# Running sums of an attention phase: from fp32 matmuls with a copied carry to float32r halves kept in PSUM

## The reference

```python
pos_cos, pos_sin = cos(pos_phases[:L]), sin(pos_phases[:L])
pos_values = x @ Wpv + bpv
pos_ret = (pos_cos * cumsum(pos_cos * pos_values, 1) + pos_sin * cumsum(pos_sin * pos_values, 1)) / sqrt(D)
key_ph = tanh(x @ Wk + bk) * pi
key_cos, key_sin = cos(key_ph), sin(key_ph)
kv_values = x @ Wkv + bkv
gh = gelu(concat([x, shift1(x)], -1) @ Wg1 + bg1)
value_gates = sigmoid(gh @ Wg2 + bg2)
kv_mem_cos = cumsum(shift1(key_cos) * kv_values * value_gates, 1)
kv_mem_sin = cumsum(shift1(key_sin) * kv_values * value_gates, 1)
gate_cumsum = maximum(cumsum(value_gates, 1), 1)
kv_ret = (key_cos * kv_mem_cos + key_sin * kv_mem_sin) / (sqrt(gate_cumsum) * sqrt(D))
bw = softmax(gelu(x @ Wb1 + bb1) @ Wb2 + bb2)
blended = bw[..., 0:1] * pos_ret + bw[..., 1:2] * kv_ret
out = x + layernorm(blended) @ Wo + bo      # normalised again, and added to the input
```

## Time and profile before

| | |
|---|---|
| median of 3 runs | 3560.59 us (3557.9 to 3568.86) |
| profiled execution | 3565.71 us, its span 3563.9 us |
| PE, DVE, ACT, POOL busy over the span | 89%, 87%, 59%, 54% |
| mean granted TensorE clock, as a share of full speed | 0.891 |
| end of the attention phase (first instruction of the next) | 802.83 us |

### The profile page before, as it was taken

One profiled execution on the slowest core, in us unless ns is written; L12 is line 12 of the kernel. 1 busy time (PEld: TensorE's weight loads), 2 busy tenths in 40 slices (PEclk: granted clock), 3 DMA queues, 4 the chain that ended last, 5 costly groups with the idle time before them and its releaser, 6 DMA issues. The chain is left out here.

```text
span 3563.9 us, 91251 instructions
## 1 busy us (share of the span) xinstructions
PE 3177.3 (89%) x31284; PEld 2733.0 (77%) x31284; DVE 3086.5 (87%) x15020; ACT 2120.2 (59%) x4411; POOL 1935.4 (54%) x1758
## 2 busy tenths in 40 slices
PE   5999999972599999999999999999999999999988
PEld 3666666642488888888888888888888888888878
DVE  5666666656999999999999999999999999999971
ACT  3444444422666666666666766666666666766662
POOL 1333333333466666556556666666556656666664
PEclk9999999986699988988888999889998888999988
DMA  2111111103333333333333333333333333333332
GB/s 64 48 54 54 54 54 54 42 30 133 141 117 117 116 105 114 122 105 105 105 105 118 125 119 119 117 108 105 124 112 105 105 105 115 124 124 117 114 117 95
DMA packets 132328, 356.85 MB, mean 100 GB/s; under 512 B 13865, under 2 KB 61609, under 8 KB 129452
## 3 DMA queue, kind: packets, MB, share of 16 engines
q1 hardware_dynamic: 131868, 351.03, 30.3%
HBM read 309.01 MB, written 25.17 MB: 94 GB/s over the span
## 5 line engine op out<-in xcount | busy, mean ns | idle before, releaser
L1209 PE MATMUL b_ps_a<-b_wup,b_hid 128*128 128x256 f32 x4096 | 955.8, 379 | 1.5 <-POOL b_hid L1023 1.5
L1198 PE MATMUL b_ps_h<-b_xT_hi,b_wd_split 128*128 128x256 f32 x4096 | 931.9, 311 | 22.7 <-ACT b_hid L1349 22.5
L1209 PEld LDWEIGHTS b_ps_a<-b_wup,b_hid 128*128 128x128 f32 x4096 | 744.3, 190 | 85.7 <-POOL b_hid L1023 1.7
L1023 POOL TENSOR_TENSOR b_hid<-b_hid,b_gates 128x512 f32<-128x512 f32 x512 | 661.9, 1295 | 197.8 <-ACT b_hid L1349 197.8
L1198 PEld LDWEIGHTS b_ps_h<-b_xT_hi,b_wd_split 128*128 128x128 f32 x4096 | 703.5, 200 | 38.3 <-issue 27.9
L1328 ACT ACTIVATE b_ohq<-b_q_no,b_minus_qid 80x128 f16<-80x128 f16 x2048 | 648.7, 391 | 1.0
L1004 POOL TENSOR_SCALAR b_rstd<-b_mv 128x2 f32<-128x2 f32 x64 | 136.4, 2131 | 860.8 <-DVE b_mv L1388 860.8
L1123 PE MATMUL b_ps_s<-b_ohr,b_ohq 80*128 80x32 f16 x16384 | 452.6, 185 | 167.1 <-issue 125.5
L1198 PE MATMUL b_ps_h<-b_xT_lo,b_wd_split 128*128 128x256 f32 x2048 | 596.9, 291 | 0.0
L1123 PEld LDWEIGHTS b_ps_s<-b_ohr,b_ohq 80*128 80x128 f16 x16384 | 443.8, 102 | 176.0 <-issue 132.3
L1349 ACT ACTIVATE b_hid<-b_ps_h 128x512 f32<-128x512 f32 x512 | 303.8, 593 | 371.5 <-PE b_ps_h L1198 371.3
(11 more groups left out here) (192 smaller groups left out, 5508.8 us busy)
## 6 DMA issues: line engine op xcount, KB each, us to landing
b_wd_split<-wd_parts SPq DMA_DIRECT2D x512, 512.0 KB, 3.8
a_keysh<-a_key SPq DMA_DIRECT2D x16, 896.0 KB, 5.4
a_x<-in_x SPq DMA_DIRECT2D x16, 512.0 KB, 4.9
x_between<-a_y SPq DMA_DIRECT2D x16, 512.0 KB, 3.2
b_x<-x_between SPq DMA_DIRECT2D x32, 256.0 KB, 2.7
wd_parts<-b_wd_split SPq DMA_DIRECT2D x16, 512.0 KB, 2.9
b_x1t<-x_between SPq DMA_DIRECT2D x32, 256.0 KB, 5.5
out<-b_y SPq DMA_DIRECT2D x32, 256.0 KB, 5.6
```

Source lines behind the costliest of these rows:

```text
L1023: G.tensor_tensor(hid[:, p % 4, :, :], hid[:, p % 4, :, :], gates[:, 2 * p:2 * p + 2, :], ALU.mult).then_inc(mix_done, 1)
L1198: mm = T.matmul(hbank[p % 2][:, j * C:(j + 1) * C], a, c, start=i == 0, stop=i == len(parts) - 1)
L1209: mm = T.matmul(abank[:, t * D:(t + 1) * D], hid[:, p % 4, j, t * P:(t + 1) * P], wup[:, 2 * p + j, :], start=p == 0 and j == 0 and t == 0 ...
```

## The change

Six things change, all in `attention_phase`.

1. The sums stay in PSUM. DVE still makes `u`; ACT casts it to float32r (`u_hi`), POOL subtracts to get what is left (`u_lo`, also float32r), and PE adds both halves with a float32r triangle `upto`. The carry is no copy any more: the banks already hold the tile's running sums, and before the next tile a float32r matrix `rest` (ones minus triangle) adds to each row the terms of the tile before that are still missing from it. The banks are started anew only at the head of a sequence. `keep_carry` and `carry` are gone.
2. Chunks go through one sequence and then the other, so `cs` is made for every chunk: 16 times, not 8.
3. The phases are loaded one turn later and first in SP's turn, and `reduce_phases(n + 1)` stands directly ahead of `gate_values(n + 1)`.
4. `terms(n + 1, 0)` and `values(n + 1, 0)` are made at the end of turn `n`, no longer at the start of the next. In ACT's turn the key waves go behind `turn_blend`.
5. `norm_out`, `add_input` and `store` of a chunk move to the next turn. On DVE `norm_out(n - 2)` now stands behind the last `blend` of `n - 1`.
6. The second half of `gate_values` becomes `gate_shares`, behind `back(n, 2)`: three steps for four. `gate_factors` takes two steps for three, and `gate_sums` clamps straight from PSUM.

```diff
-        j, b = divmod(n, seqs)
+        b, j = divmod(n, per_seq)
...
         def sums(n, t):
-            i = g % 2
-            first = j == 0 and t == 0
-            pe.wait_ge(u_done, g + 1)
+            first = g % (per_seq * TA) == 0
+            pe.wait_ge(upto_done, 1)
             if g:
                 pe.wait_ge(prod_done, g)
-            for h in range(2):
-                mm = T.matmul(cbank[h][:, :], tri[:, :], u[:, i, h * 512:(h + 1) * 512], start=True, stop=first)
             if not first:
                 for h in range(2):
-                    mm = T.matmul(cbank[h][:, :], last_row[:, :], carry[:, b, h * 512:(h + 1) * 512], start=False, stop=True)
+                    for part in (u_hi, u_lo):
+                        mm = T.matmul(cbank[h][:, :], rest[:, :], part[:, (g - 1) % 2, h * 512:(h + 1) * 512], start=False, stop=False,
+                                      skip_group_check=True)
+                mm.then_inc(rest_pe, 1)
+            pe.wait_ge(u_lo_done, g + 1)
+            for h in range(2):
+                for part in (u_hi, u_lo):
+                    mm = T.matmul(cbank[h][:, :], upto[:, :], part[:, g % 2, h * 512:(h + 1) * 512], start=first and part is u_hi,
+                                  stop=part is u_lo, skip_group_check=True)
             mm.then_inc(sums_pe, 1)
...
+        def low_terms(n, t):
+            g = n * TA + t
+            i = g % 2
+            pool.wait_ge(u_hi_done, g + 1)
+            G.tensor_tensor(u_lo[:, i, :], u[:, i, :], u_hi[:, i, :].bitcast(F32), ALU.subtract).then_inc(u_lo_done, 1)
...
-        def keep_carry(n, t):
+        def high_terms(n, t):
             g = n * TA + t
-            b = n % seqs
-            act.wait_ge(sums_pe, g + 1)
-            for h in range(2):
-                op = S.copy(carry[96:128, b, h * 512:(h + 1) * 512], cbank[h][96:128, :])
-            op.then_inc(carry_done, 1)
+            act.wait_ge(u_done, g + 1)
+
+            if g >= 2:
+                seq_tiles = per_seq * TA
+                if (g - 1) % seq_tiles == 0:
+                    act.wait_ge(sums_pe, g - 1)
+                else:
+                    act.wait_ge(rest_pe, g - 1 - (g - 1) // seq_tiles)
+            S.copy(u_hi[:, g % 2, :], u[:, g % 2, :]).then_inc(u_hi_done, 1)
...
         def gate_factors(n):
             dve.wait_ge(groot_done, n + 1)
-            V.scalar_tensor_tensor(z[:, :, 1:3], z[:, :, 1:3], 1.0 / 16, den[:, 1, :].unsqueeze(2).to_broadcast([P, TA, 2]),
-                                   ALU.mult, ALU.mult).then_inc(zscale_done, 1)
-            dve.wait_ge(zscale_done, n + 1)
             if n >= 2:
                 dve.wait_ge(blend_done, (n - 1) * TA)
-            V.tensor_copy(fac[:, n % 2, 0, :], z[:, :, 1])
-            V.tensor_tensor(fac[:, n % 2, 1, :], z[:, :, 2], zmax[:, :], ALU.mult).then_inc(fac_done, 1)
+            V.scalar_tensor_tensor(fac[:, n % 2, :, :].rearrange("p c t -> p t c"), z[:, :, 1:3], 1.0 / 16,
+                                   den[:, 1, :].unsqueeze(2).to_broadcast([P, TA, 2]), ALU.mult, ALU.mult).then_inc(zscale_done, 1)
+            dve.wait_ge(zscale_done, n + 1)
+            V.tensor_tensor(fac[:, n % 2, 1, :], fac[:, n % 2, 1, :], zmax[:, :], ALU.mult).then_inc(fac_done, 1)
...
+        def gate_shares(n):
             dve.wait_ge(exp_done, n + 1)
-            V.tensor_scalar(den[:, 0, :], z[:, :, 0], 1.0, None, ALU.add)
-            V.tensor_tensor(den[:, 1, :], z[:, :, 1], z[:, :, 2], ALU.add).then_inc(den_done, 1)
+            dve.wait_ge(constants, 1)
+            V.tensor_reduce(den[:, :, :].rearrange("p c t -> p t c"), z4[:, :, :].rearrange("p t (c k) -> p t c k", k=2), AX.X,
+                            ALU.add).then_inc(den_done, 1)
```

More of the change, by code:

```diff
@@ L138, in attention_phase @@
         sem(f"a_{n}") for n in ("w_high", "xT_hi", "x_before", "tanh", "th_abs", "key"))
[L139 to L143, removed]
+    hidden_done, exp_done, u_hi_done, lnT_done, ph_abs_done, cs_done = (
+        sem(f"a_{n}") for n in ("hidden", "exp", "u_hi", "lnT", "ph_abs", "cs"))
+    xT_pe, keys_pe, hidden_pe, logits_pe, gcum_pe, values_pe, rest_pe, sums_pe, lnT_pe, wo_pe = (
+        sem(f"a_{n}_pe") for n in ("xT", "keys", "hidden", "logits", "gcum", "values", "rest", "sums", "lnT", "wo"))
     N_WEIGHTS = 16
@@ L203, in store @@
             sp.dma_start(rows_of(x1_dram, where(n)[2]), y[:, :, :]).then_inc(x1_out, 16)
-        for n in range(-2, chunks + 1):
+        for n in range(-2, chunks + 2):
+            if has(n + 1):
+                load_phases(n + 1)
             if has(n + 2):
@@ L219, in pool_program @@
         G.memset(ones3[:, :], 1.0)
[L220 to L223, removed]
+        G.memset(key_end[:, :, :, :], 0.0)
+        G.memset(z4[:, :, 0:1], 1.0)
+        G.memset(zeros[:, :], 0.0).then_inc(constants, 1)
         def root(i, n):
@@ L253, in add_input @@
             G.tensor_tensor(y[:, :, :], y[:, :, :], x[:, n % 4, :, :], ALU.add).then_inc(x1_done, 1)
-        for n in range(-2, chunks + 1):
+        for n in range(-2, chunks + 2):
+            if has(n):
+                low_terms(n, 1)
+            if has(n - 2):
+                add_input(n - 2)
             if has(n - 1):
@@ L270, in pool_program @@
                 gate_root(n + 1)
-            if has(n - 1):
-                add_input(n - 1)
     def pe_program(pe):
@@ L448, in pe_program @@
                 project_out(n - 1)
+            if has(n + 1):
+                values(n + 1, 0)
             if has(n):
@@ L745, in norm_out @@
             op.then_inc(norm_done[2], 1)
-        for n in range(-2, chunks + 1):
+        for n in range(-2, chunks + 2):
             if has(n):
-                terms(n, 0)
                 terms(n, 1)
+            if has(n + 1):
+                turn_x(n + 1)
             if has(n - 1):
                 blend(n - 1, TA - 1)
-            if has(n + 1):
-                turn_x(n + 1)
+            if has(n - 2):
+                norm_out(n - 2)
             if has(n):
@@ L781, in dve_program @@
                 project_out(n - 1)
+            if has(n + 1):
+                terms(n + 1, 0)
             if has(n):
@@ L785, in dve_program @@
                 gate_sums(n + 1)
-            if has(n - 1):
-                norm_out(n - 1)
     with nc.Block() as block:
```

131 lines of the change are left out of this document (68 added, 63 removed).

## The result

The changed kernel takes 3580.9 us (median of 5 runs, 3579.5 to 3583.9) against 3560.7 (5 runs, 3557.9 to 3569.0): ratio 1.0047, interval 1.0036 to 1.0059. It is slower by 20 us as the medians have it and by 13 to 21 as the interval has it. The two profiled executions lie 14 us apart (spans 3577.9 and 3563.9). Forecast: 3587.

A forecast was written before the change was run, and what follows sets the result against it. PE bounds the kernel before; afterwards a chain through the engines sets the turn: 42.9 us, 45.1 with `add_input`, 47.6 with the clock. Turns +29, start -6, end +4: +27, forecast 3587 us, range 3522 to 3606.

The forecast's parts named there:

- The chain: Attention turn across PE, ACT, POOL and DVE: steps released one by another, 42.9 us with nothing in the way.
- T0: End of PE's `turn_blend(n - 1)` in turn `n`, from which the steps are counted; next one at 42.3 us before handovers.
- The handovers: Some fourteen passes between engines in a turn, at 0.03 to 0.08 us each: 0.6 us.
- `add_input`: On POOL as DVE starts the factors: holds their four-column second step, bounds nothing and 2.2 us, taken as 2.2.
- Rival 2: About even: four-column step slips past `add_input` or gap too short for the clock; 3557 us, chance 0.24.
- `norm_out`: Four DVE instructions after the last blend, held midway by POOL's low part of tile 1: 1.4 + 2.35 us.
- The clock: PE behind its new gap runs at a lower clock: 1.7 to 3.4 us a turn, taken as 2.5.
- Start and end: Outside the 13 turns: start -6 us (reductions, no `norm_out` yet), end +4 (last blend waits for two low parts).
- What costs nothing: Eight more phase reductions, waves, loads and the shorter gate chain lie off the path, with 2 us of cover.
- rival 1: Slower, as summed, with both surcharges: 47 to 48.5 us a turn, 3572 to 3604; chance 0.45.
- rival 4: Much slower: one more meeting of DVE and POOL on the path each turn, +30 us, 3617; chance 0.07.
- Rival 3: Faster: chain shorter or both surcharges absent; 42.9 us a turn, 3526, decided below 44.7; chance 0.24.

The follow-up runs named there:

- Experiment 7: Changed kernel with POOL's low-part subtraction on 16 of 1024 columns, PE's matmuls all kept: 3470.0 us, ratio 0.9744 to the kernel before.
- experiment 1: Changed kernel with the two factor steps (`gate_factors`) moved behind `back(n, 0)` on DVE: 3545.8 us, ratio 0.9953 to the kernel before.
- experiment 10: Changed kernel with the low parts of tiles 3 and 0 made by DVE, POOL keeping tiles 1 and 2: 3518.7 us, ratio 0.9884.
- experiment 2: Changed kernel with `norm_out` moved behind `back(n, 0)` on DVE, the factors still ahead of it: 3592.0 us, ratio 1.0080.
- experiment 3: Changed kernel with both the factors and `norm_out` moved behind `back(n, 0)` on DVE: 3553.2 us, ratio 0.9972.
- experiment 4: Changed kernel with `values(n, 2)` computed four times to fill PE's gap, nothing left out: 3562.8 us, ratio 1.0001.
- experiment 8: Changed kernel with the factors behind `back(n, 0)`, plus `values(n, 2)` computed twice to fill part of PE's gap: 3538.1 us, ratio 0.9935.
- experiment 6: Changed kernel with every second turn's phase reductions and wave steps done on 16 columns only: 3576.1 us.
- experiment 5: Kernel with factors and `norm_out` behind `back(n, 0)`, plus `add_input` moved behind `root(1)` and tile 0's gather on POOL: 3545.9 us, ratio 0.9958.
- experiment 12: Kernel with tile 0's low part on DVE and factors behind `back(n, 0)`; tile 3's low part returned to POOL, `values(n, 2)` ahead of `sums(n, 0)`: 3496.4 us.

## Why the prediction was right, and where its sizes were off

**The chain.** The theory was that a turn is one latency chain from T0, through two low parts, to `back(n + 1, 0)`. The turn at T0 = 404.46 shows it, and the sums of the second tile start 32.5 to 32.8 us behind T0 in all 13 turns. Us behind T0, forecast without the clock and measured:

| step ended | forecast | measured |
|---|---|---|
| cast of the last tile | 6.5 | 6.5 |
| gather of tile 2 | 11.2 | 11.2 |
| terms of the next tile 0 | 16.0 | 16.0 |
| gather of tile 3 | 23.1 | 23.1 |
| `norm_out` | 27.2 | 26.9 |
| `back(n + 1, 0)`, with `add_input`'s 2.2 | 32.8 | 32.3 |
| next T0, clock and handovers in | 47.6 | 45.9 (47.1 in the turn before) |

Experiment 7 shows the cause: without the low parts' time, and with the same matmuls, the turn is 39.5 and PE is the bound. Experiments 1 and 10 show the same from two sides. PE ran out of work at about 26.6 us (forecast 26.4) and stood idle for 5.9 in 12 of the 13 turns, within the 4.3 to 6.5 of the forecast. Left out was that the clock falls behind the first tile's wait as well, in chunk 8's turn; it costs the chain nothing, since PE has that time.

**The handovers.** This term was mis-sized. I added 0.6 us on top, but the durations in the rows overlap by 0.03 to 0.1 us where one instruction follows another, and that pays for the handovers.

**`add_input`.** I took 2.2 us, the upper bound, for a step of four columns, which no row had shown. Measured: 2.32 for 0.16. Rival 2, in which it slips past `add_input`, did not come in any of the 13 turns. The Trainium skill ("SBUF — State Buffer", section "SBUF: two separate sides") has DVE instructions with two SBUF inputs and GpSimd's exclude each other for a whole instruction, without a lower size; the trace agrees at four columns.

**`norm_out`.** Forecast 1.4 + 2.35, measured 3.4: the low part began 0.5 us behind the first of the four, and only what is left of it counts. Its own removal was worth nothing by itself (experiments 2 and 3).

**The clock.** I took 2.5 us, a choice between the bounds of 1.7 and 3.4. It cost 2.0: from the second tile's sums to the next T0 the change takes 13.9 us a turn, and 11.9 where the gap is filled (experiments 4 and 8). Of the 1.2 us between forecast and measured turn, 0.6 is the handovers, 0.3 the steps up to these sums (32.5 for 32.8) and 0.3 what follows them (13.9 for 14.2).

**How good the forecast was.** The turn came within 1.2 us of 47.6, but the change of the turn is what decides, and that was forecast at 2.2 us and measured at 1.04. Over 13 turns it is 29 us forecast and 13.5 measured. All errors of the sum went one way, towards slower.

**Start and end.** Start: forecast -6, measured -7.1 (gates of chunk 2 at 134.09 for 141.19). End: forecast +4, measured +3.4 (74.8 us from the last gates to the second phase, 71.4 before). Together with the turns, +13.5, the attention phase is 9.9 us longer, where the forecast had 27. The profiled executions differ by 4 us more, in the second phase, which is unchanged: it takes 2761.1 us before and 2765.2 after, and between 2760.9 and 2763.2 in the twelve experiments. So that part looks like scatter. The medians differ by more than the traces, 20 us; the profiled execution of the kernel before lay 5 us above its median, and what made it so isn't settled. So about half of the 20 us is accounted for by the chain, and that the median came within 6 us of 3587 is in part luck.

**What costs nothing.** The doubled phase work, the loads and the shorter gate chain: right for the phase work (experiment 6); the other two were not tried alone. It is no longer so where DVE's work comes later behind T0. In experiments 2, 3, 5, 8 and 12 the reductions or the gate step behind them meet a low part and delay `back(n, 2)`.

**The chances.** They do not add up: rival 1 (0.45, all of its range slower) and rival 4 (0.07) make 0.52 for slower with no part of rival 2, not 0.49, and leave 0.19 for the same.

**Rival 3** (faster, if the chain is under 44.7) needs the two factor steps moved: experiment 1. **My misses** in experiments 2, 3, 5, 8 and 12 have one reason: I shortened the chain on the path and took the rest as before. A second chain (`norm_out`, `add_input`, `root(1)`, `blend_norm`, terms, reductions, `back(n, 2)`) is nearly as long, and each move, on PE too, changed which instructions meet.

## What to carry to other kernels

When work is taken off the bounding engine, follow one turn through every engine in its written order; here that gave the turn to 1.2 us of 47 and the sign of the change, though not its size, while busy shares would have promised a gain of 95 us. Work that is handed to a slower engine costs its latency each time it stands between two others, so put the pieces that lie on the chain where they take least (1.22 us on DVE, 2.35 on POOL) and leave the others. Before moving an instruction, ask not only who waits for it but what it stands beside: in experiments 2 and 12 an order that ought to have been shorter lost, since it put a DVE instruction beside a POOL one or behind a wait of POOL's. And count a gap over all turns before you build on it: the turn read for experiments 8 and 12 was the one that begins a sequence, and it has gaps that the other twelve don't have.

## What the runs showed of the hardware

- A DVE instruction of 4 columns with two SBUF inputs was held 2.3 us by a POOL one (13 of 13 turns). One of 8 columns was held too (2.34 in experiment 2), and in experiment 8 another of 4 (2.2, 12 of 13 turns). Instructions with an input from PSUM were not: in the change the two of `back` took 0.66 and 0.68 us at 442.55 and 443.13, with a low part on POOL from 442.07 to 444.47, as they do alone. Nor was `BATCH_NORM_STATS2` in experiment 5, whose four began 0.6 us ahead of the end of a low part and took 1.41.
- It holds both ways: POOL's low part took 3.09 us beside DVE's reductions, 2.35 alone, and DVE's own low part 2.01 beside a gather, 1.22 alone.
- More matmuls made the kernel faster. In the change the first matmul behind each gap of 3 us and more took 0.75 to 0.77 us, for 0.47 at full clock (14 of 14; the granted clock behind two of them was 0.50, the 1.2 GHz level); behind one of 0.3 in experiment 4 the sums ran at full rate. The length of the gap does not settle it: in experiment 10 it is 3.4 us in all 13 turns, and the first matmul behind it took 0.47 to 0.50 us in seven and 0.60 to 0.77 in six. What does settle it is open.
